# A decoder's layer-0 attention stream: the cross attention of one batch placed ahead of the last self attention

## The reference

```python
x = _layernorm(x + _L0_attn_ref(x, Wq, Wk, Wv, Wo))          # 16 heads of 16, rope, causal
x = _layernorm(x + _L0_xattn_ref(x, ctx, ctx, gamma))        # 8 heads of 32, no mask
x = _layernorm(x + _L0_ffn_ref(x, w_up, w_down))
x = _layernorm(x + _L1_attn_ref(x, ...))                     # 32 heads, window
x = _layernorm(x + _L1_xattn_ref(x, tokens, ctx, ctx, ctx))  # experts by token
x = _layernorm(x + _L1_ffn_ref(x, ...))                      # routed experts
```

## Time and profile before

| | before |
|---|---|
| median of 3 runs | 986.9 us (981.38 to 987.19) |
| the profiled execution | 990.47 us, its span 988.6 us |
| TensorE busy | 823.9 us (83%) |
| VectorE busy | 589.8 us (60%) |
| ScalarE busy | 439.7 us (44%) |
| GpSimd busy | 421.3 us (43%) |
| mean granted TensorE clock | 0.909 of full speed |

### The profile page before, as it was taken

How to read it: one execution, slowest core, us unless ns; L and a number is a source line. 1 busy time by engine, 2 the same in 40 slices (tenths; PEclk the granted TensorE clock), 3 DMA queues, 4 the chain that set the end, 5 groups by cost and what they waited for, 6 DMA issues and landing times. The chain is left out here.

```text
span 988.6 us, 16377 instructions
## 1 busy us (share of the span) xinstructions
PE 823.9 (83%) x5027; PEld 504.5 (51%) x5030; DVE 589.8 (60%) x1997; ACT 439.7 (44%) x1418; POOL 421.3 (43%) x384
## 2 busy tenths in 40 slices
PE   7699999966749996999999989969973799999920
PEld 4476666644524443555555547844452455555510
DVE  3446666964757774888888871125649233333418
ACT  2366667635720002888888860001130344444512
POOL 4245545642514663666666640000002456565513
PEclk9859999987959999999999999989975799999965
DMA  9300000000004675000000000049410122222124
GB/s 330 124 1 2 1 2 1 1 1 1 1 12 113 153 186 145 1 1 1 1 2 1 2 1 1 0 157 354 129 42 1 47 72 66 74 64 70 44 81 131
DMA packets 29924, 59.76 MB, mean 60 GB/s; under 512 B 6433, under 2 KB 19117, under 8 KB 28976
## 3 DMA queue, kind: packets, MB, share of 16 engines
q1 hardware_dynamic: 20352, 41.14, 12.9%
q0 software_dynamic: 4608, 10.50, 3.4%
q10 hardware_dynamic: 4880, 7.08, 2.8%
HBM read 39.82 MB, written 8.39 MB: 49 GB/s over the span
## 5 line engine op out<-in xcount | busy, mean ns | idle before, releaser
L283 POOL TENSOR_TENSOR a_Pr<-a_Pr,a_rd 128x1024 f32<-128x1024 f32 x64 | 121.3, 1895 | 68.0 <-DVE a_rd L224 67.7
L256 ACT ACTIVATE a_Pr<-a_Sm,a_nm 128x257 f32<-128x257 f32 x256 | 127.4, 500 | 34.1 <-DVE a_nm L208 33.3
L208 DVE CUSTOM_DVE_ANT_0 a_Sm<-a_psS,table,NSK 128x256 f32<-128x256 f32 x256 | 107.9, 478 | 1.8 <-PE a_psS L157 1.8
L769 ACT ACTIVATE l_Pr<-l_Sm,l_nm 128x128 f32<-128x128 f32 (+1 forms) x192 | 88.3, 461 | 42.8 <-DVE l_nm L672 28.6
L798 POOL TENSOR_TENSOR l_Pr<-l_Pr,l_rd 128x256 f32<-128x256 f32 (+1 forms) x80 | 82.0, 1043 | 57.2 <-DVE l_rd L686 57.1
L1507 POOL TENSOR_TENSOR ro_in_tile<-ro_in_tile,table 128x384 fp32r<-128x384 f32 x4 | 7.0, 1744 | 173.0 <-DVE ro_in_tile L1566 173.0
L157 PE MATMUL a_psS<-KT,QT 64*128 64x256 f32 x512 | 74.2, 410 | 5.7 <-DVE a_nm L208 3.9
L1677 POOL DMA_INDIRECT pairs<-ex_y,ti_index x48 | 49.7, 1035 | 60.5 <-ACT ex_y L1782 50.8
L157 PEld LDWEIGHTS a_psS<-KT,QT 64*128 64x128 f32 x512 | 45.3, 190 | 57.9 <-issue 48.6
L1800 DVE TENSOR_TENSOR ex_a<-ex_psG,ex_sg 128x96 f32<-128x96 f32 x48 | 12.4, 258 | 103.1 <-ACT ex_sg L1770 84.6
L1190 PE MATMUL p_ps<-p_XT,W 128*128 128x512 f32 x160 | 72.6, 612 | 0.8 <-ACT p_XT L1203 0.8
(11 more groups left out here) (260 smaller groups left out, 1916.2 us busy)
## 6 DMA issues: line engine op xcount, KB each, us to landing
w_in<-in_w_in SPq DMA_DIRECT2D x1, 6144.0 KB, 17.4
QT<-p_E SPq DMA_DIRECT2D x64, 64.0 KB, 2.1
QT<-p_E ACTq DMA_DIRECT2D x64, 64.0 KB, 2.1
c_in<-in_c_in SPq DMA_DIRECT2D x1, 4096.0 KB, 27.4
co_G<-pairs SPq DMA_DIRECT2D x8, 512.0 KB, 7.2
W<-in_w SPq DMA_DIRECT2D x1, 3072.0 KB, 12.7
w_out<-in_w_out SPq DMA_DIRECT2D x1, 3072.0 KB, 41.2
KT<-p_E SPq DMA_DIRECT2D x32, 64.0 KB, 2.1
```

The lines of the kernel that those rows point to most:

```text
L208: nc.vector.tensor_tensor_reduce(out=Sm[:, t % 2, n, 0:S], in0=psS[:, 2 * (t % 2) + n // 2, n % 2, :], in1=mask[:, n % 2, :], scale=-scale ...
L256: nc.scalar.activation(Pr[:, t % 4, n, :], src, ACT.Exp, bias=nm[:, t % 2, n:n + 1], scale=scale if mask is None else -1.0, accum_out=den[ ...
L283: pool.tensor_tensor(p, p, rd[:, t % 2, :].unsqueeze(2).to_broadcast([P, 4, S]), ALU.mult).then_inc(normed, 1)
L769: nc.scalar.activation(Pr[:, t % 4, n, 0:n_keys], Sm[:, t % 2, n, 0:n_keys], ACT.Exp, bias=nm[:, t % 2, n:n + 1], scale=-1.0, accum_out=de ...
```

## The change

One tuple of `Layer0Plan` is written in another order. The two groups of the cross attention of batch 0 (four slots) come between the self attention of batch 2 and that of batch 3. The cross attention of batch 1, like those of 2 and 3, still follows the self attention of batch 3, and no other line differs.

```diff
     LAG = 2
 
     def __init__(self):
-        order = (("self", 0), ("self", 1), ("self", 2), ("self", 3), ("cross", 0), ("cross", 1), ("cross", 2),
+        order = (("self", 0), ("self", 1), ("self", 2), ("cross", 0), ("self", 3), ("cross", 1), ("cross", 2),
                  ("cross", 3))
         self.groups = [(kind, b, g) for kind, b in order for g in range(4 if kind == "self" else 2)]
```

## The result

The changed kernel is slower by a little over half a per cent: the ratio of its time to that of the kernel before is 1.0058, with a 95% interval of 1.0041 to 1.0075, which is 4.0 to 7.4 us. The median of 20 runs is 990.21 us (988.28 to 995.04), beside 986.26 us (981.38 to 987.90) of 20 runs before. The two medians are only 4.0 us apart since the times of each kernel fall into two clusters some 5 us apart: before, 6 of 20 runs are in the lower one (981.4 to 982.0), after, 14 of 20 (988.3 to 990.6). The ratio takes all runs. Cluster against like cluster the distance is some 7.5 us; what separates the clusters is not known, so how much of the difference lies in their shares stays open.

The account below looks back on a forecast made before the run. TensorE was taken as the fuller engine over most of the phase, with VectorE nearly full in the cross stretch. 3.6 + 0.5 + 4.5 = +8.6 us on the median 986.9 gave 995.5 us, range 987 to 1001.

Parts of the forecast that it names:

- The work itself: Whole phase: the edit only permutes slots and output projections, so TensorE's own work stays the same: 0 us.
- The new wait: At score(44), which waits for VectorE's apply of batch 3's norm in the same step: 4.7 us late.
- What comes back: In the steps behind score(44), part of the 4.7 us delay is regained, leaving +3.6 us (2.5 to 4.7).
- the moved duties: Batch 0's cross stores, measure and apply, moved to steps 30 to 34: new waits 1.6 us, net +0.5 us.
- The sign: Intervals of more than 3 us among self slots 32 to 35 would show moved duties costing more than 1.6 us.
- The clock: TensorE's clock falls once, at about score(44)'s start, for 10 us at the low clock: +4.5 us, bounds 0 to +9.
- A: Rival: behind score(44) the clock stays low to the end of the stretch; 13.1 us, 1000.0 us; chance 0.20.
- B: Rival: the clock falls at score(44) but comes back at once; 5.6 us, 992.5 us; chance 0.20.
- C: Rival: the clock doesn't fall at score(44); 4.1 us, 991.0 us; chance 0.09.
- D: Rival: score(44) waits, but its time was idle anyway through VectorE's backlog; 0 to +1 us, 987.5 us; chance 0.08.
- E: Rival: faster, as VectorE bounds the last stretch and a quarter of its cross duties leaves it; 982.8 us; chance 0.05.

Follow-up runs that it names:

- the filled wait: Changed kernel with ten more matmuls on TensorE just ahead of score(44)'s wait for batch 3's normed rows; ratio 1.0031 (1.0019 to 1.0044) to the kernel before.

## Why the prediction was right or wrong, point by point

Forecast were +8.6 us (995.5 us) in a range of 987 to 1001; measured were +5.7 (4.0 to 7.4), and a median of 990.21 us. The total is in the range, the mechanism is the one that was forecast, and one term of the sum was too large.

**The work itself**, priced at 0: right. TensorE's and VectorE's busy times are the same within 0.4%, and from slot 15 to slot 43 the new order took 95.23 us, the old one 95.39.

**The new wait**: right in place, cause and size. Forecast were an idle stretch of 4.85 us released by the apply, and an apply of 2.29 us; measured 4.93 and 2.28. The score came 192.84 - 184.73 = 8.11 us behind its predecessor, 5.00 over the 3.11 of a cross slot. The Trainium skill's rule for the shared ports (SBUF — State Buffer, "SBUF: two separate sides") agrees with the trace again: the apply ran beside a norm of 1.97 us and took twice the 1.14 us of the earlier trace rows. Of its two instructions one took 0.38 us; the other began 0.1 us behind the norm's start, took 1.98 us and ended 0.14 us behind it. The 1.14 us that the prediction took for a fast apply held such a wait too, a short one (0.40 and 0.82 us): the median of the 16 instructions of this line is 0.41 us, so an apply that meets no norm takes some 0.8.

**What comes back, and the moved duties**: right, by the two runs that part them. The wait costs 5.00 us; of the kernel before fall away 1.09 us of waits in its last four slots, and 0.16 us up to slot 43. That makes 5.00 - 1.09 - 0.16 = 3.75 us, against 3.6 + 0.5 = 4.1 forecast. From slot 43 to slot 47 the new order without the wait took 14.10 us and with the filled wait 17.36: 3.26 us for the wait, against 3.6 forecast. The duties are 14.10 - 13.53 - 0.16 = 0.4 us, against 0.5; this is near the size by which executions differ (0.48 us between the two of the changed kernel). The moved duties are visible where they were expected. The scores of slots 30 to 36:

```profile
141.43 0.92 PE L595 MATMUL l_psS<-KT,QT 32*128 32x128 f32 x8
144.33 0.92 PE L595 MATMUL l_psS<-KT,QT 32*128 32x128 f32 x8
147.45 0.92 PE L595 MATMUL l_psS<-KT,QT 32*128 32x128 f32 x8 [0.48 <-DVE l_nm L672]
150.68 0.92 PE L595 MATMUL l_psS<-KT,QT 32*128 32x128 f32 x8
153.25 0.92 PE L595 MATMUL l_psS<-KT,QT 32*128 32x128 f32 x8
156.04 0.92 PE L595 MATMUL l_psS<-KT,QT 32*128 32x128 f32 x8 [0.36 <-DVE l_nm L672]
159.27 1.13 PE L595 MATMUL l_psS<-CTX,X 32*128 32x256 f32 x8
```

Three of the intervals are over 3 us, two of them among slots 32 to 35, which I had named as a sign that the duties cost more than 1.6 us there. The sign was badly chosen: from slot 31 to slot 36 it is 14.94 us, 2.6 over five self slots of 2.46, where the load behind an output had cost 1.75. So the duties added some 0.9 us. They come back in the cross slots, so that the order is even by slot 43, and the run without the wait (1.0015) agrees.

**The clock**: right that it falls once, at about the time of score(44) (between 191.5 and 191.7 us, the score at 192.84). Wrong in the size, and this is the mis-sized term. I took 10 us at the low clock and 4.5 us of loss. It lasted 6.6 us and more, 1.1 of it still idle, and cost the interval behind score(44) 5.71 - 3.11 = 2.6 us; the filled wait puts the same fall at 2.7 us by the ratios, and at 2.2 to 2.7 by the stage. Forecast with 2.6 in place of 4.5, the sum is 6.7 us, inside the measured 4.0 to 7.4; as written it was 8.6, just above it. In the profiled execution the absent fall in the tail gave another 1.3 us back (19.54 - 18.28), but in the repeat it was there. One reading of the rows was wrong as well: the prediction set the stall 24 us ahead of the last score and let that much work follow it at the low clock. 24.34 us lie between slot 40 and slot 47; behind score(44) there are only three slots, 9.91 us before and 11.94 after. The term's upper bound of 9 us, and with it A's 13.1, leans on that figure. Of the Trainium skill's rule, that the clock is given back soon after TensorE is busy again (TensorE: Matmul & The Clock Gate, "What's actually happening"), the runs show both sides: 3.3 us in the variant with the sooner apply, 6.6 in the changed kernel, 13.5 in the old order with the late apply. The rule was nearer than my 10 us for the change itself.

**The rivals.** B, a clock that comes back at once, with 5.6 us, was nearest to the measured 5.7; it would not be right to say that it won by its mechanism, since the fall lasted twice as long as it assumed. A and C are excluded for the two profiled executions of this kernel, where the clock fell and was back after 6.6 us; D by the stage, where 3.26 us of the wait stay with the clock's fall taken out; and E by the run without the wait.

**What stays open.** Why the clock is given back after 3.3 us in one kernel and after 13.5 in another, behind nearly the same slots, isn't settled. The runs show only that filling the idle stretch takes the fall away, each in one profiled execution. The share of the fall (2.7 us) rests on two ratios whose intervals overlap, and on the timelines, which agree. What makes the two clusters of times wasn't looked for.

## What to carry to other kernels

When work is reordered in a software pipeline, list for each moved piece the step at which its result is written and the step at which it is first read: here no resource became scarcer, but a slack of four steps became none, and the price could be read off the old trace by laying the producer's finish over the consumer's start. Add to such a wait what the clock does behind it, and look for idle stretches of TensorE that are already there: at the seams of two phases, a few filler matmuls were worth 0.7% of this kernel (0.5 to 1.0), as much as the whole reordering moved.

## What the runs showed of the hardware that I had not expected

- A long gap isn't needed for the clock to fall. With the seam filled it fell 0.5 us behind the end of a gap of 1.26 us; with the gaps of the filling pipeline filled too, it stayed at 1.00 up to 209 us.
- The same gap brings the fall in one execution and not in another: behind 2.10 us of idleness in the tail the clock fell in the repeat of the changed kernel, and stayed at 1.00 in its first profile.
- Matmuls whose results nobody reads keep the clock up, even with an operand of zeros (`nothing`): behind 4.58 us of them score(44) ran at 1.00.
- The length of a low stretch varied from 3.3 to 13.5 us behind idle stretches of 2.5 to 4.9 us, not in step with their length: 2.75 us and 4.93 us of idleness were both followed by some 6.6 us at 0.50, and 4.90 us by 13.5.
